# Cross-attention with a mixture of experts: value matmuls that stream their columns twice, and routing moved between the two halves of an odd round's softmax

## The reference

```python
x = x + xattn(layernorm(x), ctx, ...)      # 16 heads of 16, 77 keys each
x = x + ffn(layernorm(x), ...)

# xattn
q = (x @ Wq + bq).reshape(bs, n_ctx, HEADS, d)
kv = (data @ Wkv + bkv).reshape(bs, n_data, HEADS, 2 * d)
attn = softmax(einsum('bqhd,bkhd->bhqk', q, k) * scale)
out = einsum('bhqk,bkhd->bqhd', attn, v).reshape(bs, n_ctx, WIDTH) @ Wp + bp

# ffn: 8 experts, each token goes to its best 2
xf = layernorm(x, ln_g, ln_b)
scores, idx = top_k(xf @ router_w, 2)
gate = softmax(scores)
for e in experts:
    h = layernorm(xf, g, b)
    h = clip(h @ W1 + b1 ...) * silu(clip(h @ W2 + b2, -20, 20))
    acc += gate[:, e] * clip(clip(h) @ Wo + bo)
```

## Time and profile before

| | us |
|---|---|
| median of 3 runs | 940.02 |
| lowest and highest | 939.27 and 948.33 |
| the profiled execution | 937.55 |
| its span | 935.8 |
| TensorE busy in the span | 888.0 |
| VectorE busy | 743.5 |
| ScalarE busy | 645.2 |
| POOL busy | 412.6 |

### The profile page before, as it was taken

How to read it: one execution, slowest core, us unless ns; L and a number is a source line. 1 busy time by engine, 2 the same in 40 slices (tenths; PEclk the granted TensorE clock), 3 DMA queues, 4 the chain that set the end, 5 groups by cost and what they waited for, 6 DMA issues and landing times.

```text
span 935.8 us, 19131 instructions
## 1 busy us (share of the span) xinstructions
PE 888.0 (95%) x6174; PEld 797.1 (85%) x6174; DVE 743.5 (79%) x1757; ACT 645.2 (69%) x1297; POOL 412.6 (44%) x649
## 2 busy tenths in 40 slices
PE   4999999999989998999999999999999999999995
PEld 3888887888878787888999999898898998998994
DVE  2678888888888889787979887886877877778783
ACT  3666766667676764766968777766776777677773
POOL 3555576777776666340432331505214234052052
PEclk9899999999999999999999999999999999999998
DMA  5332342342345337643755464827817737466442
GB/s 143 66 68 48 63 97 66 80 103 66 63 126 186 109 128 258 183 116 118 220 142 176 126 170 149 242 91 186 295 29 227 270 75 260 170 179 182 141 79 27
DMA packets 132368, 129.17 MB, mean 138 GB/s; under 512 B 59936, under 2 KB 117152, under 8 KB 132128
## 3 DMA queue, kind: packets, MB, share of 16 engines
q1 hardware_dynamic: 119392, 110.36, 38.8%
q0 software_dynamic: 12864, 17.44, 10.2%
HBM read 102.01 MB, written 25.36 MB: 136 GB/s over the span
## 4 chain that ended last, share of the span: by engine, by line
PE 82%; DVE 7%; issue 4%; ACT 3%; POOL 2%; SPq 1%; DMA 1%; POOLq 0%; another core or an unknown queue 0%; DVEq 0%; ACTq 0%
PE bank L1974 36%; PE bank L2018 19%; PE bank L1807 6%; PE bank L1737 4%; PE bank L1966 3%; PE bank L1784 3%; PE bank L1755 3%; PE bank L1774 2%; PE bank L2006 2%; PE bank L1943 1%; DVE maxes L1238 1%; PE bank L1792 1%; PE bank L1819 1%; DVE probs L1244 1%; PE bank L1830 1%
## 5 line engine op out<-in xcount | busy, mean ns | idle before, releaser
L852 POOL DMA_INDIRECT out_rows<-yo,token x68 | 113.7, 1672 | 382.8 <-ACT yo L1095 316.0
L1974 PE MATMUL bank<-xh,wh 128*128 128x512 f32 (+1 forms) x672 | 234.5, 349 | 3.2 <-DVE gate_in L1610 2.6
L1974 PE MATMUL bank<-xl,wh 128*128 128x512 f32 (+1 forms) x672 | 228.7, 340 | 0.0
L1974 PE MATMUL bank<-xh,wl 128*128 128x512 f32 (+1 forms) x672 | 228.2, 340 | 0.0
L1586 DVE TENSOR_TENSOR wl<-raw,wh 128x1024 fp32r<-128x1024 f32 x126 | 152.5, 1220 | 13.4 <-ACT wh L1026 12.4
L2018 PE MATMUL bank<-wh,hh 128*128 128x256 f32 x496 | 141.7, 286 | 1.5 <-issue 1.5
L1974 PEld LDWEIGHTS bank<-xh,wh 128*128 128x128 f32 x672 | 128.1, 191 | 17.2 <-DVE gate_in L1610 4.5
L2018 PE MATMUL bank<-wh,hl 128*128 128x256 f32 x496 | 140.5, 283 | 1.0 <-issue 1.0
L2018 PE MATMUL bank<-wl,hh 128*128 128x256 f32 x496 | 140.4, 283 | 1.0 <-issue 1.0
L1974 PEld LDWEIGHTS bank<-xh,wl 128*128 128x128 f32 x672 | 127.7, 190 | 14.9
L1974 PEld LDWEIGHTS bank<-xl,wh 128*128 128x128 f32 x672 | 128.2, 191 | 10.8
(11 more groups left out here) (195 smaller groups left out, 1868.6 us busy)
## 6 DMA issues: line engine op xcount, KB each, us to landing
raw<-in_W SPq DMA_DIRECT2D x42, 1024.0 KB
raw<-in_Wo SPq DMA_DIRECT2D x25, 1024.0 KB
whole<-in_W SPq DMA_DIRECT2D x8, 1024.0 KB, 6.8
xs<-in_x SPq DMA_DIRECT2D x32, 128.0 KB, 2.4
out_rows<-x SPq DMA_DIRECT2D x32, 128.0 KB, 1.8
shared<-z_rows SPq DMA_DIRECT2D x7, 520.0 KB
bo_row<-in_bo SPq DMA_DIRECT2D x25, 128.0 KB
k_blocks<-k_parts SPq DMA_DIRECT2D x128, 19.2 KB
```

Source lines behind the costliest of these rows:

```text
L852: e.indirect_dma_start(out=out, out_offset=bass.IndirectOffsetOnAxis(ap=token[j % 4][:, s:s + 1], axis=0), in_=yo[j % 2][:, s, :], in_offs ...
L1974: mm = e.matmul(ps[:, h * cols:(h + 1) * cols], ws[split_before(j) % 2][:, w, c, m * P:(m + 1) * P], xx[j % 2][:, c, 0:cols], start=(h == ...
```

## The change

Two edits. In `values`, a matmul whose block begins at head 2 or later writes its columns twice, in one instruction: once where they belong, and once from column 272 on, which nothing reads. The moving operand is read twice for that, through a dimension with step 0. Blocks 0 and 1 do not have the room, so 8 of 10 matmuls are doubled: 34 columns become 68 and 51 become 102. In VectorE's list, in odd rounds, `best_experts(i - 6)` and `route` stand behind the first half's subtraction and xf_sums, ahead of gate_norm and the second half. In even rounds `best_experts` stays.

```diff
--- before.py
+++ after.py
@@ -1534,6 +1534,11 @@
                     xf_sums(i - 4)
                 if i == NT - 1:
                     low_rows(0)
+                if not even and 0 <= i - 6 < NT:
+                    best_experts(i - 6)
+                p = (i - 7) // 2
+                if not even and 0 <= p < PAIRS:
+                    route(p)
                 p = (i - 9) // 2
                 if not even and 0 <= p < PAIRS:
                     if p < LATE_GATES:
@@ -1570,11 +1575,8 @@
                     x_variance(i + 5)
                 if 0 <= i - 1 < NT:
                     normalized(i - 1)
-                if 0 <= i - 6 < NT:
+                if even and 0 <= i - 6 < NT:
                     best_experts(i - 6)
-                p = (i - 7) // 2
-                if not even and 0 <= p < PAIRS:
-                    route(p)
                 if i == EARLY_TILES + 6:
                     early_counts()
 
@@ -1793,6 +1795,17 @@
                                      ident)
                 mm.then_inc(xn_t_mm, 1)
 
+            def twice(at, moving):
+
+
+
+                size, n = moving.shape
+                step = HEADS * VW - at
+                if at + 2 * step > 512:
+                    return value_bank[:, at:at + n], moving
+                out = value_bank[:, at:at + 2 * step].rearrange("p (r c) -> p r c", r=2)
+                return out[:, :, 0:n], moving.unsqueeze(1).broadcast_to([size, 2, n])
+
             def values(i):
                 b = i // 2
                 if i:
@@ -1804,10 +1817,10 @@
                         e.wait_ge(probs_t_out, 3 * i + k // 4 + 1)
                     first, nh = block_heads(k)
                     size = P if k < KB - 1 else TAIL
-                    mm = e.matmul(
-                        value_bank[:, first * VW:(first + nh) * VW], probs_t[i % 2][0:size, k, :],
-                        v_blocks[b % 2][0:size, k, 0:nh, :].rearrange("p j d -> p (j d)"),
-                        start=(k == 0), stop=(k == KB - 1), skip_group_check=True)
+                    out, moving = twice(first * VW, v_blocks[b % 2][0:size, k, 0:nh, :].rearrange(
+                        "p j d -> p (j d)"))
+                    mm = e.matmul(out, probs_t[i % 2][0:size, k, :], moving, start=(k == 0),
+                                  stop=(k == KB - 1), skip_group_check=True)
                 mm.then_inc(values_mm, 1)
 
             def route_logits(i):
```

## The result

Timed beside each other, the kernel before has a median of 941.44 us and the changed one 947.99: a ratio of 1.0061 (95% interval 1.0038 to 1.0084), 5.7 us slower (3.6 to 7.9), where I had forecast 1.9 less. The profiled execution took 954.06 us, its span 952.3.

The account below looks back on a forecast made before the run. The prediction took TensorE, busy 95% of the span, as the bound, with VectorE counting only where TensorE waits for it. Terms -6.3 + 1.6 + 0.3 + 1.8 + 0.4 + 0.3 gave -1.9 us: 938.1 from 940.0, range 933.9 to 943.5.

Parts of the forecast that it names:

- -6.3: Attention rounds 8 to 30: moving the group removes all of TensorE's waits for VectorE's subtraction, -6.3 us (bounds 0 and -6.3).
- The nine waits: Rounds 8 to 30: TensorE's score matmuls wait nine times for VectorE's subtraction, 6.3 us in all, 1.1 the longest.
- What is late next is TensorE itself: Steady rounds: with the subtraction up to 1.5 us earlier, TensorE itself is the next limit, so all 6.3 us is gained.
- I price the later half at nothing: Odd rounds 7 to 25: the softmax's second half starts 0.1 to 0.5 us later, covered by ScalarE, at no cost.
- +1.6, +0.3, +1.8, +0.4: Costs in us: q_l of round 27, q_l of round 29, first gate matmul of round 31, then rounds 33 to 37.
- weighed only for round 31: Rival, chance 0.08: TensorE idles 2.3 us in round 31 and a second low-clock spell costs 1.7 us.
- The doubled columns, "+0.3": Value matmuls of 32 tiles: weight loads set the pace, so extra columns are nearly free, +0.3 us.
- the rival of the paid columns: Value matmuls of all tiles: every doubled column costs time, +16 us, 956; chance 0.06.
- the case that the nine waits bring nothing: Steady rounds: the waits stay under another name, at transposes, exponentials or attn; +4.4 us, 944.4; chance 0.12.
- The better clock: First expert tile: the 1.2 GHz spell near 330 us goes and round 31's delay is absorbed; -5.4 us, 934.6; chance 0.2.

Follow-up runs that it names:

- move_only: The kernel before with only the moved group in VectorE's odd rounds, columns written once: 950.81 us against 939.47, ratio 1.0102.
- twice_only: The kernel before with only the doubled columns, VectorE's old order: 942.37 us, ratio 1.0005.
- early_only: The kernel before with the group moved in odd rounds up to 25 only, columns once, on another chip: 933.99 us against 934.42, ratio 1.0002.
- late_only: The kernel before with the group moved only in odd rounds from 27 on, columns once: 946.9 us against 942.3, ratio 1.0059.
- puts_next_round: move_only with all four of POOL's scatters of a pair issued together one round later: 954.12 us against 942.3 of the kernel before, ratio 1.0175.
- split_puts_before: The kernel before with the second tile's two scatters one round later, pairs 0 to 8: 936.5 us against 939.47, ratio 0.9976.
- split_puts_move: move_only with the second tile's two scatters one round later for pairs 0 to 8: 942.8 us, ratio 1.0033 to the kernel before.
- split_puts_after: The whole change with the second tile's two scatters one round later, pairs 0 to 8: 942.87 us against 942.3 of the kernel before, ratio 1.0012.
- split_limited: split_puts_move with the group moved only up to round 25: 936.74 us against 942.3 of the kernel before, ratio 0.9953.
- split_limited_b: The same kernel as split_limited in another group of runs: 936.92 us against 941.42 of the kernel before, ratio 0.9966.
- split_limited_twice: split_limited with the doubled columns too, on the other chip: 934.72 us against 934.42 of the kernel before, ratio 1.0008.
- split_all_limited: split_limited with pairs 9 and 10 split as well, on the other chip: 943.31 us against 934.42 of the kernel before, ratio 1.0089.

## Why the prediction was wrong

All profiles in four stretches, in us, between the first maxima (L1238) of rounds 0, 8 and 26, the first gate matmul and the end; in the last column what of rounds 8 to 25 ran at 1.2 GHz:

| | 0 to 7 | 8 to 25 | 26 to gate | to the end | low |
|---|---|---|---|---|---|
| before | 64.9 | 161.5 | 54.4 | 633.7 | 0 |
| the change | 62.5 | 172.5 | 60.2 | 636.4 | 17.1 |
| move_only | 67.7 | 167.2 | 59.2 | 635.5 | 10.2 |
| twice_only | 66.4 | 168.9 | 54.0 | 633.4 | 10.2 |
| early_only | 66.0 | 159.6 | 56.5 | 629.4 | 3.4 |
| late_only | 65.0 | 163.1 | 58.4 | 635.0 | 0 |
| puts_next_round | 62.3 | 165.2 | 66.6 | 636.0 | 3.4 |
| split_puts_before | 63.6 | 158.8 | 55.2 | 633.0 | 0 |
| split_puts_move | 63.8 | 158.8 | 58.9 | 636.3 | 0 |
| split_puts_after | 65.0 | 159.5 | 61.3 | 634.5 | 0 |
| split_limited | 64.2 | 159.4 | 56.8 | 633.7 | 0 |
| split_limited_b | 63.8 | 157.7 | 58.2 | 633.6 | 0 |
| split_limited_twice | 69.7 | 159.5 | 56.7 | 633.3 | 0 |
| split_all_limited | 69.5 | 159.6 | 60.5 | 632.5 | 0 |

**The step that failed: "-6.3", the steady rounds.** The nine waits did go, and brought next to nothing. "What is late next is TensorE itself" was wrong for a good part: other engines stand close behind. The plainest measure is the kernels with the split, in which VectorE has no held results: rounds 8 to 25 take 158.8 us in the old order (`split_puts_before`) and 158.8 and 159.5 with the move, where in the old order the subtraction still costs TensorE five waits, 2.6 us; in their place stand short waits for q_t, attn, raw and logits. With the move only up to round 25 they take 159.4 and 157.7. Over the runs `early_only` measures 0.0 us (2.5 less to 2.9 more) for the step that I had at -6.3. The gain of 2.0 to 2.7 us that split kernels with the move show against before in this stretch is had by the split without the move as well. I took the list's total for the gain and did not ask how far the other engines stand behind TensorE.

The second half of the step is "I price the later half at nothing". It named ScalarE's exponential as cover, since ScalarE had waited 1.71 us at the logits copy. That wait was a held result itself: TensorE had ended the logits at 151.87, and ScalarE copied them at 154.68, 1.02 behind the fourth scatter. I used it as slack and did not ask what made it. And the second half's results have a second reader, VectorE, which the later half brings beside the scatters. Where results are held this turns the step's 0 into a loss, 4 us by the estimate above.

That held results make TensorE wait is shown in the trace (round 21), and with the split they go, and with them 0.7% of the time (1.0102 to 1.0033, with intervals that overlap). That they are all of this difference is argued, and so is that they explain each spell at 1.2 GHz: in `twice_only` 10.2 us of them stand in rounds 8 to 25 without any move.

**The late rounds, "+1.6, +0.3, +1.8, +0.4": right in kind, perhaps too small.** TensorE waits 3.26 for q_l of round 27 (3.33 in `late_only`) instead of 0.77, +2.5 against 1.6. The group itself takes 1.53 there (267.53 to 269.06). The other 0.9 lies in the small operations behind it, from gate_norm to the second maxima, which take 2.4 us in place of 1.4: one of the early table's takes 0.77 instead of 0.17, another 0.42 instead of 0.15. Why they stretch is not shown. The clock fell in that wait, which I had weighed only for round 31; but kernels with the split and the old order here have a spell at this place too (260.5 to 263.9 in `split_puts_before`, behind a wait of 2.0). The gate matmul waits 1.56 instead of 0.45, +1.1 against 1.8, and there the clock stayed at 1.00. From round 26 to the gate `late_only` takes 4.0 more than before against the 3.7 priced, and 1.3 more behind it against 0.4. By the runs it is 5.6 us (2.7 to 8.5) against 4.1, and this is the largest part of the change's 5.7 us. With the scatters split a difference of that kind shows too: 1.0033 with the late rounds, 0.9953 without.

**The doubled columns, "+0.3": right.** Next to nothing at 2.4 GHz, and 1.0005 over the runs (3.2 us less to 4.2 more); the rival of the paid columns (956) is out, although the first profile's time looked like it.

**Rivals.** The nearest was the case that the nine waits bring nothing (944.4, chance 0.12), though not quite by its mechanism: the waits came back under other names, but only short ones, and the rest was held results and the clock. The better clock did not come. The range ended at 943.5: I had left out the worse half of this case, and priced it without the late rounds' clock.

Sum as measured: 0.0 for the steady rounds, 5.6 for the late ones, 0.5 for the columns, 6.1 against 5.7 for the whole. That it comes out so near is in part luck, since the 0.0 is from a run without held results and the change's own profile has them; with the estimate of 4.0 in its place the sum is 10.1, above the 7.9 that the interval of the whole allows. Each term is uncertain by some 3 us, so the runs don't settle the shares. What stays open: what holds TensorE's results beside the scatters, and why one profile of the same instructions has them and another, from another chip, has none.

## What to carry to other kernels

The total of a list of waits bounds a gain from above; the gain itself ends where the next engine stands, and a kernel in which the waits are gone and nothing else is held up (here the move with two scatters at a time, beside the same without the move) shows where that is. An idle stretch of an engine is slack only if one knows what ends it. Before moving work ahead of an operation, look up who else reads its result and what runs on GpSimd at that time: in round 21, 0.1 us later was 3 us later. Where a list of odd rounds is changed, price the rounds that carry extra work by themselves, with the clock behind their waits; here they were the largest part of the loss, and leaving them out of the move was the remedy. And an experiment that moves one thing can delay another: two of the kernels here with later scatters lost their time at a load that needs what is scattered.

## What the runs showed of the hardware

In the profile of the change, results of TensorE that ended beside the later ones of four indirect scatters in a row on GpSimd were read up to 3.2 us late, 0.9 to 1.2 us behind the end of the third or the fourth scatter (210.57 to 213.78, with the fourth's end at 212.75; in `puts_next_round` 161.40 to 164.13, with 163.04). VectorE and ScalarE were held alike. In the one profile of four in a row from another chip, results that ended beside the third and the fourth were read at once (241.88 to 241.91). With two in a row VectorE had no such wait. In a value tile, 20 records with up to 102 columns take 2.28 us and with up to 51 columns 2.26 at 2.4 GHz, 4.17 to 4.36 and 4.11 at 1.2 GHz. In the changed kernel a wait of 1.28 us was followed by 3.4 us at 1.2 GHz, one of 1.56 us in front of the gate matmul by none.
